# Compact level blocks, an output copy on ScalarE and a low-rank gate in a gated-linear-attention and feed-forward kernel

## Reference

```python
xn = layernorm(x)
q, k, v = xn @ Wq * 64**-0.5, xn @ Wk, xn @ Wv      # 4 heads; 64 key, 128 value features
g = log_sigmoid(xn @ gk_w1 @ gk_w2 + gk_b) / 16     # gk_w1 256x16, gk_w2 16x256
S = exp(g_t)[:, None] * S + k_t[:, None] * v_t; o_t = q_t @ S    # per head, token by token
o = o * rsqrt(mean(o*o) + eps) * rms_w * silu(xn @ Wg)
x = x + layernorm(o @ Wo)
# feed-forward: expert e has sequences 2e and 2e+1; 256 -> 1024 -> 256
x = x + layernorm(gelu(layernorm(x) @ w1[e] + b1[e]) @ w2[e] + b2[e])
```

## Time and profile before

| | us |
|---|---|
| median of 3 runs | 1289.01 |
| the profiled execution, its own time | 1290.03 |
| its span, first to last instruction | 1288.2 |
| PE busy / VectorE busy / ScalarE busy / GpSimd busy | 1215.7 / 1019.7 / 718.4 / 627.2 |
| one call with all three streams (645.44 to 721.14) | 75.7 |

### The profile page before, as it was taken

How to read it: one execution, slowest core, us unless ns; L and a number is a source line. 1 busy time by engine, 2 the same in 40 slices (tenths; PEclk the granted TensorE clock), 3 DMA queues, 4 the chain that set the end, 5 groups by cost and what they waited for, 6 DMA issues and landing times.

```text
span 1288.2 us, 24042 instructions
## 1 busy us (share of the span) xinstructions
PE 1215.7 (94%) x8628; PEld 1040.1 (81%) x8628; DVE 1019.7 (79%) x2404; ACT 718.4 (56%) x1539; POOL 627.2 (49%) x893
## 2 busy tenths in 40 slices
PE   5889999999999999999999999999999999999957
PEld 3678888878888788878888788887888888788856
DVE  3769788897978969798787978889697987979663
ACT  5365565656456564654756555566646646565423
POOL 5336443563545544564445635356454654456431
PEclk9989999999999999999999999999999999999988
DMA  3110010100101001010011001010010100101000
GB/s 99 39 33 18 18 46 5 54 18 18 50 18 50 6 17 50 21 51 1 18 50 54 17 18 50 1 54 18 18 50 22 50 1 18 50 22 34 2 17 17
DMA packets 31781, 38.31 MB, mean 30 GB/s; under 512 B 2448, under 2 KB 29104, under 8 KB 31664
## 3 DMA queue, kind: packets, MB, share of 16 engines
q1 hardware_dynamic: 31136, 36.25, 8.4%
q10 hardware_dynamic: 528, 0.52, 0.1%
HBM read 28.38 MB, written 8.39 MB: 29 GB/s over the span
## 4 chain that ended last, share of the span: by engine, by line
PE 74%; DVE 18%; issue 4%; POOL 2%; ACT 1%; DMA 0%; POOLq 0%; DVEq 0%; SPq 0%
PE ps_big L254 16%; PE ps_big L256 15%; PE ps_big L255 15%; PE ps_level L298 7%; PE ps_out L456 5%; DVE attn_T L582 3%; PE ps_out L459 3%; DVE q_blockdiag L592 3%; PE ps_level L305 2%; DVE bn L639 2%; PE ps_state L438 2%; PE ps_transpose L470 2%; PE ps_level L254 2%; PE ps_level L256 2%; PE ps_level L255 2%
## 5 line engine op out<-in xcount | busy, mean ns | idle before, releaser
L1059 POOL TENSOR_TENSOR k_decayed<-k_decayed,block_totals 128x256 f32<-128x256 f32 x192 | 157.5, 821 | 266.6 <-PE ps_level L298 166.5
L298 PEld LDWEIGHTS ps_level<-q_blockdiag,k_decayed 128*128 128x128 f32 x1280 | 163.3, 191 | 46.6 <-DVE q_blockdiag L592 38.6
L298 PE MATMUL ps_level<-q_blockdiag,k_decayed 128*128 128x128 f32 x1280 | 173.8, 280 | 25.3 <-DVE q_blockdiag L592 24.2
L582 DVE COPY_PREDICATED attn_T<-level_masks,ps_level 128x512 f32<-128x512 uint32 x160 | 152.3, 952 | 23.7 <-PE ps_level L298 23.7
L1065 POOL TENSOR_TENSOR rstd<-rstd,minus_half 128x1 f32<-128x1 f32 x192 | 112.4, 588 | 108.3 <-DVE rstd L643 108.3
L592 DVE TENSOR_TENSOR q_blockdiag<-q_blockdiag,block_totals 128x512 f32<-128x512 f32 x192 | 139.1, 725 | 19.5 <-PE ps_level L305 19.5
L254 PE MATMUL ps_big<-w_ff_hi,h_hi 128*128 128x256 f32 x512 | 150.4, 294 | 0.0
L255 PE MATMUL ps_big<-w_ff_lo,h_hi 128*128 128x256 f32 x512 | 144.5, 282 | 0.0
L256 PE MATMUL ps_big<-w_ff_hi,h_lo 128*128 128x256 f32 x512 | 144.4, 282 | 0.0
L846 ACT ACTIVATE ps_transpose<-ps_big,ff_b_cols 128x512 f32<-128x512 f32 x128 | 84.7, 662 | 79.9 <-PE ps_big L256 78.9
L630 DVE SCALAR_TENSOR_TENSOR o<-o,o_rstd,out_gate 128x128 f32<-128x128 f32 x256 | 93.2, 425 | 45.1 <-POOL o_rstd L1080 45.1
(11 more groups left out here) (115 smaller groups left out, 3232.8 us busy)
## 6 DMA issues: line engine op xcount, KB each, us to landing
w_raw<-L_ffn_w SPq DMA_DIRECT2D x16, 1024.0 KB, 5.9
out<-y SPq DMA_DIRECT2D x16, 512.0 KB, 2.9
x_in<-L_attn_x SPq DMA_DIRECT2D x15, 512.0 KB, 3.9
ff_b_rows<-L_ffn_b SPq DMA_DIRECT2D x8, 128.0 KB, 2.2
x_in<-L_attn_x ACTq DMA_DIRECT2D x1, 512.0 KB, 4.0
w_raw<-L_attn_Wv SPq DMA_DIRECT2D x1, 512.0 KB, 5.7
w_raw<-L_attn_Wg SPq DMA_DIRECT2D x1, 512.0 KB, 6.9
y<-L_attn_Wo SPq DMA_DIRECT2D x1, 512.0 KB, 7.9
```

Source lines behind the costliest of these rows:

```text
L298: last = nc.tensor.matmul(PL[tl][:, c * CH:(c + 1) * CH], kk[:, tl, c * CH:(c + 1) * CH], q[:, :, :, 1, :], start=True, stop=True)
L582: nc.vector.copy_predicated(dst, m.to_broadcast([P, 2 * NCH, HC // h, h]), src)\
L1059: nc.gpsimd.tensor_tensor(k, k, t.to_broadcast([P, n, h]), ALU.mult)\
```

## The change

Levels 0 to 4 compute only what lies inside blocks of 32 tokens: for each chunk four matmuls of 32 keys by 32 columns, written to four partition groups of `PL[tl]`, 128 columns wide in all. `copy_pairs` puts them into a compact matrix `AC` (128 partitions, 8 chunk-and-heads, 32 columns), `copy_diag` puts the own token's product there as well (head-sum columns are arranged for that), and ScalarE's `expand` copies the blocks of `AC` into `Am`. `dg` and `o_part` go; ScalarE copies the bank `PO` to `o` (`o_evac`), before `squares`, whose scratch is half as wide with waits for it. The gate is computed as two products: `gd` (256 to 16 columns, hi and lo parts side by side in 128 columns) into `PL[0]`, ScalarE's copy to `gr` and VectorE's `lowrank_lo`, then `gl(tl)` with one matmul each into `PL[1 - tl]`. `kp(0)` stands between `gd` and `gl`; the orders on ScalarE and VectorE change with it. Once, at the start, the gate's weights are placed by five small DMAs instead of two, zeroed and split, and the masks are folded to 32 columns; the matmuls that made gk_w1 gk_w2 go.

The core of the diff:

```diff
+        AC = sb("attn_blocks", [P, KT, NCH * 2, BS])
...
+        G1 = [sb(f"w_gate_down_{n}", [P, KT, P], F32R) for n in ("for_hi", "for_lo")]
+        G2 = sb("w_gate_up", [P, D], F32R)
+        gr = sb("gate_lowrank", [P, T], F32R)
...
                         if i < MASKED:
-                            q = qbd[:, tl, :, c * CH:(c + 1) * CH].rearrange("p a (n t h) -> p a n t h", t=2, h=h)
-                            last = nc.tensor.matmul(PL[tl][:, c * CH:(c + 1) * CH],
-                                                    kk[:, tl, c * CH:(c + 1) * CH], q[:, :, :, 1, :],
-                                                    start=True, stop=True)
+                            for g in range(CH // BS):
+                                t = slice(c * CH + BS * g, c * CH + BS * (g + 1))
+                                q = qbd[:, tl, :, t].rearrange("p a (n t h) -> p a n t h", t=2, h=h)
+                                last = nc.tensor.matmul(PL[tl][BS * g:BS * (g + 1), c * BS:(c + 1) * BS],
+                                                        kk[:, tl, t], q[:, :, :, 1, :], start=True, stop=True)
                             continue
...
+                def gd():
+
+                    if not B and not C:
+                        pe.wait_ge(c_glo, 2)
+                    pe.wait_ge(sem["dv_xlo"], at("dv_xlo", n, KT))
+                    if B:
+                        pe.wait_ge(sem["ac_cp"], at("ac_cp", s, 12))
+                    for kt in range(KT):
+                        nc.tensor.matmul(PL[0][:, :], G1[0][:, kt, :], xT_hi[:, kt, :], start=(kt == 0), stop=False)
+                        last = nc.tensor.matmul(PL[0][:, :], G1[1][:, kt, :], xT_lo[:, kt, :], start=False,
+                                                stop=(kt == KT - 1))
+                    last.then_inc(sem["pe_gd"], 1)
+
                 def gl(tl):
+
+                    pe.wait_ge(sem["dv_gr"], at("dv_gr", n, 1))
+                    nc.tensor.matmul(PL[1 - tl][:, :], G2[:, tl * P:(tl + 1) * P], gr[:, :], start=True, stop=True)\
+                        .then_inc(sem["pe_gl"], 1)
+
+                def kp(tl):
                     if not B and not C:
                         pe.wait_ge(c_lo, 1)
-                    pe.wait_ge(sem["dv_xlo"], at("dv_xlo", n, KT))
                     if C:
                         pe.wait_ge(sem["dv_y4"], at("dv_y4", p, 3 + tl))
                     elif B:
                         pe.wait_ge(sem[("ac_v", "ac_g")[tl]], at(("ac_v", "ac_g")[tl], s, NCH))
-                    feature_tile(PB[tl], 2 * D + tl * P).then_inc(sem["pe_gl"], 1)
-
-                def kp(tl):
+                    feature_tile(PB[tl], D + tl * P).then_inc(sem["pe_k"], 1)
...
                 def att(c):
-                    pe.wait_ge(sem["dv_cp"], at("dv_cp", s, 2 * MASKED))
+                    pe.wait_ge(sem["ac_ex"], at("ac_ex", s, 4 * KT))
                     pe.wait_ge(sem["ac_cp"], at("ac_cp", s, 12))
                     pe.wait_ge(sem["dv_qu"], at("dv_qu", s, 2 * NL))
                     pe.wait_ge(sem["ac_v"], at("ac_v", s, c + 1))
                     if c:
-                        pe.wait_ge(sem["dv_o"], at("dv_o", s, c * H))
+                        pe.wait_ge(sem["ac_o"], at("ac_o", s, c))
...
+                    if c < 2 and A:
+                        pe.wait_ge(sem["dv_gl"], at("dv_gl", n, KT))
...
                     kh(0)
                     kh(1)
                 if A:
+                    gd()
+                if B:
+                    st(0)
+                    att(0)
+                if A:
+                    kp(0)
                     gl(0)
                     gl(1)
-                if B:
-                    st(0)
-                    att(0)
-                if A:
-                    kp(0)
                     kp(1)
                 if B:
                     st(1)
...
+                    if i > 2:
+                        dve.wait_ge(sem["dv_c0"], at("dv_c0", s, tl + 1))
+                    dst = AC[:, tl, :, :].rearrange("p a (n t h) -> p a n t h", t=2, h=h)[:, :, :, 1, :]
+                    src = PL[tl][:, 0:NCH * BS].rearrange("p (a n h) -> p a n h", a=2 * NCH, h=h)
                     m = masks[:, i, :].bitcast(U32).rearrange("p (a n h) -> p a n h", a=1, h=h)
-                    nc.vector.copy_predicated(dst, m.to_broadcast([P, 2 * NCH, HC // h, h]), src)\
+                    nc.vector.copy_predicated(dst, m.to_broadcast([P, 2 * NCH, BS // (2 * h), h]), src)\
                         .then_inc(sem["dv_cp"], 1)
+
+                def copy_diag(tl):
+
+                    dve.wait_ge(sem["pe_diag"], at("pe_diag", s, 1))
+                    dve.wait_ge(sem["dv_cp"], at("dv_cp", s, 5 + tl))
+                    m = dmask[:, :].bitcast(U32).rearrange("p (a r) -> p a r", a=1)
+                    src = PO[:, CH:2 * CH].rearrange("p (a r n) -> p a n r", a=2 * NCH, n=1)[:, :, :, tl]
+                    nc.vector.copy_predicated(AC[:, tl, :, :], m.to_broadcast([P, 2 * NCH, BS]),
+                                              src.to_broadcast([P, 2 * NCH, BS])).then_inc(sem["dv_c0"], 1)
...
-                def o_part(c):
-                    dve.wait_ge(sem["pe_att"], at("pe_att", s, c + 1))
-                    if c >= 2:
-                        dve.wait_ge(sem["pe_ogt"], at("pe_ogt", s, c - 1))
-                    elif c == 0:
-                        dve.wait_ge(sem["dv_dg"], at("dv_dg", s, 1))
-                    for hd in range(H):
-                        w = slice(hd * HV, (hd + 1) * HV)
-                        nc.vector.scalar_tensor_tensor(o[:, c % 2, w], v[:, c, w], dg[:, c * H + hd:c * H + hd + 1],
-                                                       PO[:, w], ALU.mult, ALU.add).then_inc(sem["dv_o"], 1)
...
+                def lowrank_lo():
+                    dve.wait_ge(sem["ac_gr"], at("ac_gr", n, 1))
+                    r = slice(2 * GB, 3 * GB)
+                    nc.vector.tensor_tensor(gr[r, :], PL[0][r, :], gr[r, :].bitcast(F32), ALU.subtract)\
+                        .then_inc(sem["dv_gr"], 1)
+
                 def gates(tl):
                     dve.wait_ge(sem["ac_abs"], at("ac_abs", n, tl + 1))
-                    nc.vector.tensor_scalar(gm[:, tl, :], PB[tl][:, :], gkb[:, tl:tl + 1], 0.0,
+                    nc.vector.tensor_scalar(gm[:, tl, :], PL[1 - tl][:, :], gkb[:, tl:tl + 1], 0.0,
                                             ALU.add, ALU.min).then_inc(sem["dv_gl"], 1)
...
+                        if step in (4, 5):
+                            copy_diag(step - 4)
...
+                        const_lo(1)
+                    lowrank_lo()
                 if C:
                     normed_y(3)
                 if A:
+                    gates(0)
                     gates(1)
                 if B:
-                    o_part(0)
                     state(0)
                     og(0)
-                    o_part(1)
                     state(1)
                 if A:
                     gate_sub()
                     og_lo(0)
                     og(1)
                     state(2)
-                    o_part(2)
                     ln2(0)
                     og_lo(1)
-                    o_part(3)
                     og(2)
                     normed_attn(0)
                     ln2(1)
...
+                def expand(tl):
+
+                    act.wait_ge(sem["dv_cp"], at("dv_cp", s, 2 * (MASKED - 1) + tl + 1))
+                    act.wait_ge(sem["dv_c0"], at("dv_c0", s, tl + 1))
+                    for g in range(CH // BS):
+                        r = slice(BS * g, BS * (g + 1))
+                        copy(Am[r, tl, :, r], AC[r, tl, :, :], "ac_ex")
+
+                def o_evac(c):
+                    act.wait_ge(sem["pe_att"], at("pe_att", s, c + 1))
+                    if c >= 2:
+                        act.wait_ge(sem["pe_ogt"], at("pe_ogt", s, c - 1))
+                    copy(o[:, c % 2, :], PO[:, :], "ac_o")
+
                 def squares(c):
-                    act.wait_ge(sem["dv_o"], at("dv_o", s, H * (c + 1)))
-                    if c:
-                        act.wait_ge(sem["ac_sq"], at("ac_sq", s, H * c))
+                    act.wait_ge(sem["ac_o"], at("ac_o", s, c + 1))
                     for hd in range(H):
-                        nc.scalar.activation(junk[:, hd * HV:(hd + 1) * HV], o[:, c % 2, hd * HV:(hd + 1) * HV], ACT.Square,
+                        if hd >= 2:
+                            act.wait_ge(sem["ac_sq"], at("ac_sq", s, H * c + hd - 1))
+                        elif c:
...
+                    if B and step in (10, 11):
+                        expand(step - 10)
...
                 if A:
+                    act.wait_ge(sem["pe_gd"], at("pe_gd", n, 1))
+                    copy(gr[:, :], PL[0][:, :], "ac_gr")
+                if B:
+                    o_evac(0)
+                    squares(0)
+                if A:
                     for tl in range(KT):
```

(51 more changed lines are left out.)

121 lines of the change are left out of this document (71 added, 50 removed).

## The result

The changed kernel takes 1255.47 us in the median of 6 runs (1250.8 to 1260.4) beside 1289.05 for the kernel before: a ratio of 0.974 (95% interval 0.972 to 0.977). The forecast was 1258, with a range of 1232 to 1286. The profiled execution took 1255.89 us (span 1254.1).

What follows compares the result with a forecast made beforehand. TensorE (busy 94%) was taken as the bound, VectorE setting the first stage's pace. 14 rounds at -2.9 + 1.4 give -21 us; round 0 -3.5, start -1, last -6: -31.5 from 1290.0, less 1.0, forecast 1258, range 1232 to 1286.

Steps and rivals of the forecast that it cites:

- level step, old kind to new: TensorE, levels 0 to 4: one level's cost falls from 0.88 to 0.62 us, a gain of 0.27 a step.
- `f1(0)` after the first level: First stage: shorter VectorE copies bring `f1(0)` 1.2 and 0.7 us earlier, less where GpSimd also splits weights.
- first stage, a round: Levels part of a round: 1.3 us from VectorE's copies, 1.6 from six level steps on TensorE, -2.9 us.
- `st(1)` after the gate's first record: Gate path: `st(1)` waits 1.35 us for `state(0)` and starts at 692.1, `gd` starting at 684.80.
- `gd` to `att(3)`: Second stage: a span of 20.3 us (18.9 before), `att(3)` waiting about 0.7 us for the output copy.
- second stage, a round: From `gd` on: +1.4 us a round, through ScalarE's output copies; bounds -1.4 to +3.
- 14 full rounds: Both stages, -2.9 and +1.4 us a round, over 14 full rounds: -21 us.
- round 0, start, last rounds: Outside the full rounds: round 0 -3.5 us, start -1, last -6.
- the rival of 1302: Levels on TensorE: small matmuls cost by the record, a level 1.10 us, 1302 in all, slower; chance 0.09.
- The gate's saving: Gate projections on TensorE: 2.8 us become 1.4; the 1.4 saved are spent waiting 1.35 us for `state(0)`.
- ScalarE's chain holds `att(3)`: Second stage: `att(3)` waits for ScalarE's `o_evac(2)`, starting at 705.15 against 703.73 before.
- The rival that nothing new binds: ScalarE and VectorE keep up, the gate saving stays: about 1216, or 1237 without one wait; chance 0.22 together.

Runs made afterwards that it cites:

- levels_twice: The changed kernel with every matmul of levels 2 to 4 issued twice: 1287.65 us.
- levels_only: The changed kernel with the gate path (matmuls and place in the orders) of the kernel before: 1258.36 us.
- state_first: The changed kernel with `state(0)` ahead of `gates(0)` and `gates(1)` on VectorE: 1247.99 us.
- copy2_early: The changed kernel with ScalarE's copy of chunk 2's output ahead of the output gate's Silu: 1242.34 us.
- both_orders: The changed kernel with state_first's and copy2_early's edits together: 1228.44 us.
- all_orders: The changed kernel with both_orders' edits and GpSimd's second feed-forward weight splits (j = 1) at steps 3, 5, 7, 9 instead of 1 to 4: 1218.78 us.

## Why the prediction was right

| term | predicted | measured in the profiled executions |
|---|---|---|
| level step, old kind to new | 0.88 to 0.62 | 0.88 to 0.59; steps 1.98 apart |
| `f1(0)` after the first level | 1.2 (j = 0), 0.7 (j = 1) earlier | 1.63 (6.88 to 5.25) and 1.60 (7.66 to 6.06) |
| first stage, a round | -2.9 | -3.74 (j = 0), -2.47 (j = 1) |
| `st(1)` after the gate's first record | 7.3, wait 1.35 | 7.30, wait 1.24 |
| `gd` to `att(3)` | 20.35, wait 0.75 | 20.59, wait 0.77 (1.6 in j = 1) |
| second stage, a round | +1.4 | +1.9 |
| 14 full rounds | -21 | -20.4 |
| round 0, start, last rounds | -3.5, -1, -6 | -3.8, -1.9, -8.0 |
| sum | -31.5 | -34.1 |

The mechanism of each step held. The small matmuls run in four groups side by side: four records of 32 columns take 0.034 us, four of level 5's 64 columns 0.057 (the prediction had 0.03 and 0.06), and levels_twice gives 9 ns a record, so the rival of 1302 is out. The gate's saving is spent on the wait for the state: levels_only and state_first show it from both sides. One reading in it was wrong: `state(0)` is not "now queued behind both gates", it stood behind them before too. What changed is that the gates are ready later: the second `Abs` ends 3.74 us after the first gate record in the kernel before and 5.96 us after it now. ScalarE's chain holds `att(3)`: shown by copy2_early. The copy of chunk 2 ends 20.33 us after `gd` began, as worked out (20.3), and `att(3)` starts 0.26 us later.

The rival that nothing new binds did not come true here, and its price was too high: with both waits gone both_orders takes 1228 and not 1216. Its rounds with j = 0 gain 1.8 us and not 2.8, since `ogt(1)` then waits 0.95 us. That all_orders (1219) is close to 1216 is chance; 9.7 us of it come from the later splits, which that rival did not have.

Three sizes were off, and by luck their errors cancelled. First, the copies of levels 0 and 1 freed more than I took. A copy of 128x128 lets the next operation start after 0.23 us (it was 1.1); I took 0.35, and gave back 0.8 us for GpSimd's company in j = 1 where all of it was gained. Second, the second stage cost 0.5 us more, +1.9 for my +1.4, of which 0.24 us lie ahead of `att(3)` (its start behind the copy) and the rest behind it. Third, the clock was not in the sum. Six falls of 1.46 us are 8.8 us that the changed kernel pays; the kernel before had two, of 0.9 us. Without falls on either side rounds with j = 1 gain 2.0 us (76.67 to 74.64); with one they gain 0.6 (76.67 to 76.1). The sum came right because the first error (0.9 us a round, falls left aside) about equals the other two (0.5 and 0.5). The last rounds gave 2.0 us more than summed; the kernel before has two stretches at the low clock there (at 1186 and 1241 us) that the changed one lacks, and what they cost is not shown.

The wait of `att(3)` was worked out as 0.75 us and is 1.6 with j = 1, which the prediction itself would have called much longer. It costs no more: `att(3)` starts 20.59 us (j = 0) and 20.58 us (j = 1) after `gd`, because ScalarE's copy sets it. With j = 0 TensorE has lost most of the difference before, at `ogt(1)`, which waits 0.59 us for `og(1)`. VectorE's four operations of `og(1)` take 2.15 us there, beside GpSimd's split of weights, and 1.14 us with j = 1, where there is none:

```profile
681.89 2.15 DVE L656 SCALAR_TENSOR_TENSOR o<-o,o_rstd,out_gate 128x128 f32<-128x128 f32 x4 [0.20 <-POOL o_rstd L1157]
...
758.00 1.14 DVE L656 SCALAR_TENSOR_TENSOR o<-o,o_rstd,out_gate 128x128 f32<-128x128 f32 x4 [0.20 <-POOL o_rstd L1157]
```

## What to carry to other kernels

Work taken off the engine that sets the end counts only up to the next thing that comes late, so follow each freed stretch to the next wait on every engine, and look at the written order there: two moved calls were worth 27 us beside the 34 us of the whole change. A cut may be worth nothing alone and 14 us once the order around it is mended, so measure it again then. And a short wait of TensorE can cost twice: look at the granted clock behind it.

## What the runs showed of the hardware

- A stretch in which TensorE is partly idle is followed by 3.4 or 6.8 us at 1.2 GHz in some rounds and not in others of the same program. One of 3.4 us costs 1.46 us in levels_only and 0.9 in the kernel before; one of 6.8 us costs 2.3 (copy2_early, 75.97 against 73.65).
- Matmuls of 32 rows by 32 columns in four partition groups cost 9 ns a record at 2.4 GHz (levels_twice) and 13 at 1.2 GHz (round 0 of the changed kernel).
- A VectorE multiplication of 128x512 takes 0.73 us alone, 1.1 beside GpSimd's key update and 1.53 beside its subtraction of 128x512; `og(1)`'s four operations of 128x128 take 1.14 us alone and 2.15 beside such a subtraction.
